# A convolutional LSTM block and a masked bottleneck block on one core: the copy of x1 to the output is issued piece by piece in the last stage

## The reference, cut to what matters

```python
# L0: ConvLSTM over the 96 rows, forward and backward, then a 1x1 projection, batch norm, ReLU
hs_f = _convlstm_scan(xr, w_f[:, :, 1, :], b_f, reverse=False)
hs_b = _convlstm_scan(xr, w_b[:, :, 1, :], b_b, reverse=True)
y = einsum('oc,bchw->bohw', w_proj, concat([hs_f, hs_b]))
x1 = relu(gamma * (y - mu) * rsqrt(var + EPS) + beta) + x       # (8, 48, 96, 96) float32
# L1: masked, channel-pruned inverted bottleneck with a residual
mask = (conv1x1(x1, w_mask) + b_mask >= 0);  mask_dilate = maxpool3x3(mask)
s = sigmoid(mean(x1) @ w_sal.T + b_sal);  vector = (s >= 144th largest of s)   # per image
h = relu(bn1(conv1x1(x1, w_pw1))) * mask_dilate * vector
h = relu(bnd(dwconv3x3(h, w_dw))) * mask * vector
h = bn2(conv1x1(h, w_pw2)) * mask
return x1 + h
```

## Time and profile before

| | |
|---|---|
| median of 3 runs | 1809.51 us (1807.85 to 1809.67) |
| the profiled execution | 1802.15 us, its span 1800.4 us |
| DVE busy over the span | 1397.2 us (78%) |
| PE busy over the span | 1627.0 us (90%) |
| last matmul of `gather` ends | 1229.2 us |
| first matmul of `bottleneck` starts | 1239.2 us |
| first depthwise tap on DVE | 1248.1 us |
| last masked result on DVE | 1789.3 us |
| four copies of x1, issue to landing | 15.7 to 55.1 us |

### The profile page before, as it was taken

The page is one execution under the profiler, slowest core; times in us unless marked ns, Lnnn a source line. Parts: engine busy times, 40 slices in busy tenths (PEclk is TensorE's granted clock), DMA queues, the critical chain, the costliest instruction groups (busy, mean ns, idle before and its releaser), DMA issues. The chain is left out here.

```text
span 1800.4 us, 43798 instructions
## 1 busy us (share of the span) xinstructions
PE 1627.0 (90%) x16562; PEld 1218.2 (68%) x16562; DVE 1397.2 (78%) x2211; ACT 1275.1 (71%) x2343; POOL 54.4 (3%) x88
## 2 busy tenths in 40 slices
PE   5999999999999999999997663457999999999996
PEld 5999999999999999999997221124333333333332
DVE  4777777777777777777776445764999999999996
ACT  4888888888888888888887343703666666666663
POOL 2000000000000000000000000000000000000000
PEclk9999999999999999999999998657999999999997
DMA  4454545455555555555553998929222222222222
GB/s 119 135 143 135 144 134 144 135 143 135 143 136 142 136 141 137 141 138 140 138 139 88 257 256 186 227 67 335 52 45 45 45 45 45 46 46 46 46 46 46
DMA packets 82904, 219.03 MB, mean 122 GB/s; under 512 B 20792, under 2 KB 26828, under 8 KB 82380
## 3 DMA queue, kind: packets, MB, share of 16 engines
q1 hardware_dynamic: 74504, 193.89, 39.7%
q0 software_dynamic: 6144, 16.52, 6.4%
q10 hardware_dynamic: 2180, 7.57, 1.9%
HBM read 98.71 MB, written 61.49 MB: 89 GB/s over the span
## 5 line engine op out<-in xcount | busy, mean ns | idle before, releaser
L1384 DVE SCALAR_TENSOR_TENSOR acc<-h1d,wt,acc 128x768 f32<-128x768 f32 x480 | 483.4, 1017 | 30.5 <-ACT acc L1295 17.3
L264 PE MATMUL gates<-state,w_high 64*128 64x384 f32 x4608 | 504.6, 337 | 0.0
L264 PEld LDWEIGHTS gates<-state,w_high 64*128 64x128 f32 x4608 | 416.8, 185 | 0.0
L1162 PE MATMUL psd<-h1p,wt 64*64 64x384 f32 x3456 | 301.2, 488 | 11.3 <-ACT h2p L1327 11.3
L264 PE MATMUL gates<-state,w_low 64*128 64x384 f32 x2304 | 267.7, 337 | 0.0
L264 PE MATMUL gates<-x_both,w_high 64*128 64x384 f32 x2304 | 237.4, 338 | 18.8 <-DVE w_low L380 18.8
L1162 PEld LDWEIGHTS psd<-h1p,wt 64*64 64x64 f32 x3456 | 126.2, 132 | 187.4 <-issue 173.3
L264 PEld LDWEIGHTS gates<-x_both,w_high 64*128 64x128 f32 x2304 | 207.6, 186 | 18.8 <-issue 18.8
L317 ACT ACTIVATE sig_f<-gates 48x384 f32<-48x384 f32 x384 | 187.0, 487 | 37.9 <-PE gates L264 33.1
L264 PEld LDWEIGHTS gates<-state,w_low 64*128 64x128 f32 x2304 | 208.8, 185 | 0.0
L411 DVE TENSOR_TENSOR h_new<-sig_o,tanh_c 128x384 f32<-128x384 f32 x192 | 107.2, 558 | 122.3 <-ACT tanh_c L335 122.3
(11 more groups left out here) (139 smaller groups left out, 1551.4 us busy)
## 6 DMA issues: line engine op xcount, KB each, us to landing
x_taps<-x_both SPq DMA_DIRECT2D x192, 195.5 KB, 3.1
x_raw<-x_steps SPq DMA_DIRECT2D x192, 192.0 KB, 3.1
h_rows<-h_new SPq DMA_DIRECT2D x192, 144.0 KB, 2.3
h_in<-h_rows SPq DMA_DIRECT2D x48, 576.0 KB, 7.4
x_last<-x_both SPq DMA_DIRECT2D x192, 98.0 KB, 2.9
out<-y SPq DMA_DIRECT2D x4, 4032.0 KB, 36.6
out<-z POOLq DMA_DIRECT2D x48, 336.0 KB, 4.9
sig_o<-x_steps SPq DMA_DIRECT2D x190, 48.0 KB, 2.0
```

The costliest lines, as they stand in the source:

```text
L264: return nc.tensor.matmul(gates[p][d][:, m, 0:NH], w[own, n, m, :], moving[own], start=start, stop=stop)
L1162: mm = nc.tensor.matmul(psd[64 * m:64 * m + 64, i, 0:NH], wt[own, to:to + 64], h1[own, dy + 4 * m:dy + 4 * m + 4, dx:dx + W], start=(tap = ...
L1384: nc.vector.scalar_tensor_tensor(a, window(h1d[d % 2], tap), par(D_UNITS[s], TAP + tap), a, ALU.mult, ALU.add).then_inc(acc_done if tap == ...
```

## The change

The four copies leave `gather`. In `bottleneck` SP issues, behind the two mask transfers of each group, the copy of x1 of this same group and chunk: 8 rows of two images, 112 partitions by 768 values, 336 KB. There are 48 of them. Each pair of images has one semaphore; from the second chunk on SP waits for the pair's copy before, and POOL waits for the copy of its own group in every chunk instead of only in the first. Only pass 0 does so.

```diff
@@ gather, sync
             n = sp.value_load(passes[0:1, 0:1], min_val=1, max_val=2)
-            for g, pair in enumerate(GROUPS):
-                sp.dma_start(out_lanes[:, pair * PX:(pair + 1) * PX],
-                             y[0:HI + C, pair].rearrange("p r w -> p (r w)")).then_inc(copied[g], 16)
             with sp.If(n > 1):
@@ bottleneck, sync, masks(o)
                         sp.dma_start(mask[n % 2][64 * half:64 * half + C], every).then_inc(mask_in[n % 2], 16)
+                    if o == 0:
+
+                        if c:
+                            sp.wait_ge(x1_copied[g], 16 * c)
+                        at = c * CPX
+                        sp.dma_start(out_lanes[:, GROUPS[g] * PX + at:GROUPS[g] * PX + at + CPX],
+                                     y[0:HI + C, GROUPS[g]].rearrange("p r w -> p (r w)")[:, at:at + CPX]
+                                     ).then_inc(x1_copied[g], 16)
@@ bottleneck, gpsimd
                     pool.wait_ge(zm_done, Z + n + 2)
-                    if o == 0 and c == 0:
-                        pool.wait_ge(copied[g], 16)
+                    if o == 0:
+                        pool.wait_ge(x1_copied[g], 16 * c + 16)
```

More of the change, by code:

```diff
@@ L817, in marks_pe, with gather @@
         return 2 + B
-def gather(nc, cst, par, w1, place, folded, wt, packs, packs_stored, passes, y, out_lanes, copied):
+def gather(nc, cst, par, w1, place, folded, wt, packs, packs_stored, passes):
     ORDER = [pair + HB * half for pair in range(HB) for half in range(2)]
@@ L1008, in _, with bottleneck @@
                 program(1)
-def bottleneck(nc, y, out_lanes, wt, packs, passes, copied, mask_rows, masks_stored):
+def bottleneck(nc, y, out_lanes, wt, packs, passes, mask_rows, masks_stored):
     NP, ND, NZ = len(P_IMAGES), len(D_UNITS), len(GROUPS)
@@ L1041, in bottleneck @@
         out_added = [sem(f"out_added{n}") for n in range(2)]
+        x1_copied = [sem(f"x1_copied{g}") for g in range(NZ)]
         pw1_done, relu1_done, prod_done, chain, acc_done, relu2_done = (
@@ L1457, in build @@
         packs_stored = ctx.enter_context(nc.semaphore("packs_stored"))
-        copied = [ctx.enter_context(nc.semaphore(f"x1_copied{g}")) for g in range(HB)]
         masks_stored = ctx.enter_context(nc.semaphore("masks_stored"))
@@ L1479, in build @@
             selection(nc, sums, folded, cst, ws, bs, par, loaded, place, passes)
-            gather(nc, cst, par, w1, place, folded, wt, packs, packs_stored, passes, y, out, copied)
-        bottleneck(nc, y, out, wt, packs, passes, copied, mask_rows, masks_stored)
+            gather(nc, cst, par, w1, place, folded, wt, packs, packs_stored, passes)
+        bottleneck(nc, y, out, wt, packs, passes, mask_rows, masks_stored)
 def kernel(x, L0_conv_w_f, L0_conv_b_f, L0_conv_w_b, L0_conv_b_b, L0_conv_w_proj, L0_conv_gamma, L0_conv_beta,
```

## The result

| | before | changed |
|---|---|---|
| median, 20 runs each | 1809.71 us (1805.71 to 1816.45) | 1805.37 us (1794.43 to 1813.42) |
| ratio | | 0.9968, 95% interval 0.9953 to 0.9983 |
| profiled execution, its span | 1802.15, 1800.4 | 1806.29, 1804.5 |

The account below looks back on a forecast made before the run. VectorE bounds the last stage, and TensorE's jump, its code fetch behind the copies, delays its start. Terms -5.6 + 0 + 0 + 0 + 0 took 1809.5 to 1803.9 us; 8-in-10 range 1799.5 to 1809.0.

Parts of the forecast that it names:

- the hole behind the gather: Between gather and first tap: TensorE idles 10.07 us, seven microseconds its own, its jump's code fetch queued behind the copies' packets.
- Step 1: TensorE's jump at the gather's end: 4.0 us instead of 9.56 once the copies leave, gain 5.6 us (4.7 to 6.6).
- Step 2: Barrier to first tap: TensorE still starts at half clock, taken as 0; catching full clock worth up to 3.1 us.
- rival A: Start of the last stage: TensorE keeps its clock, in all -8.4 us, 1801.1 us; chance 0.18.
- Steps 3 to 5: Last stage: 48 added copies, POOL's wait for its group's copy, and z's later release each cost 0.
- The sum: Whole kernel: -5.6 us with all other terms 0, bounds -9.7 to -4.0, giving 1803.9 us.
- Rival B: TensorE's jump: code fetch waits one packet's turn, or two, so gain only 1.6 to 3.2 us, 1807.1 us; chance 0.13.
- Rival C: TensorE's jump: long because of where it goes, not the copies; change worth 0, 1809.5 us; chance 0.11.
- Rival D: Last stage: copy and accumulating transfer delay each other, z late past 16.9 us landing; slower, 1827 us; chance 0.08.

## Why the prediction was right, point by point

- **What bounds the kernel, and the hole behind the gather.** Right. The jump took 9.6, 10.6, 9.5 and 9.4 us in the four profiles with large copies in flight as it began, and 5.1, 4.7, 4.7, 5.0, 4.8 and once 3.5 in the six without.
- **Step 1, the jump without the copies.** Right in kind, too optimistic in size: I took 4.0 us, the middle of 3.0 and 4.9; the changed kernel measured 5.07 and its repetition 4.99. The gain of the jump was 4.5 us instead of 5.6, the gather's 4.8. The term was mis-sized where I pieced the jump together from a packet of 0.94 us: in the changed kernel two code packets come close behind each other and are served in 1.7 and 2.5 us. With one packet it would have been near the mark: 3.5 us, once. The nearest row was TensorE's own jump at the end, 4.9 us; it should have been the value and not the bound.
- **Step 2, the clock.** The 0 was right, the reasoning was not, so this is partly luck. I had set the pause against the time to the fall as if the length of the pause decided. The clock fell 1.4 to 4.9 us after the last matmul, differently in profiles of like kernels: in the changed kernel after 1.4, sooner than in either case that I had read, without the copies after 4.7. With the shortest pause (2.5 us, second pass left out) the stage began at half clock; in the run with a jump of 3.5 us and a pause of 4.0 the clock held 0.9 us into the stage, and the first tap came 8.1 us behind the barrier instead of 9.5: rival A in small. In the five profiles with a jump of 4.7 to 5.1 us it began at half clock.
- **Steps 3 to 5, the copies in the last stage.** Right: taps 1,019 ns, 540.7 us from the first tap to the last masked result (541 forecast), no new wait, 561.5 us with and 562.1 without copies. Landing grew by 0.8 us where I had allowed 5.
- **The sum.** 1803.9 us forecast, 1805.4 measured; step 1's 1.1 us too much is about that difference, which is itself within the noise. The forecast of -5.6 us lies in the interval, -3.1 to -8.5.
- **Rival B, one packet's turn.** Denied. The code waited 6.4 to 7.2 us in the four profiles with packets of 36 KB, for the rest of one and three more, and 5.3 with 3 KB pieces, of 0.12 us each, where four would be half a microsecond. So the count holds for the large packets only, and what stands in front of the code among small ones stays open. The page "DMA: Bandwidth & Descriptors" of the Trainium skill (section "Queues, rings and completion order") says that a DMA engine changes between queues at packet boundaries and that a packet there is typically 9 to 17 descriptors. I had taken a packet of the profile for such a packet; it may be only a descriptor of one, which no run here shows. What the runs deny is a wait for one of the profile's packets, not that rule.
- **Rival C.** Denied by the repetition and by the copies' move alone (4.7 us).
- **Rival D.** Did not come: 5.7 us of landing where 16.9 would have been needed. A relative of it is real: masks behind large copies in one queue cost 3.4 us in one experiment and 19.8 in another. I had read the 29.3 us of the mask's landing and used it only as an argument for D; it also says why the copies had to be cut when they were moved.

## What to carry to other kernels

Read the drains of a barrier: they name the engine that is late, and an engine that computes nothing can be it. A jump over unused code costs a fetch through the DMA engines, so keep bulk transfers out of its microseconds, and keep them out of the queue in which small urgent ones wait: cut them and issue each behind the urgent one. When stages that did not change vary by more than the change is worth, compare stage by stage and take the total only from many runs.

## What the runs showed of the hardware that I had not expected

- A far jump of TensorE takes 4.7 to 5.1 us (once 3.5) with no copy in flight, and 9.4 to 10.6 us beside large copies, with one of these in flight as with three, and from SP's queue as from ScalarE's. The code stood behind the rest of one packet of 36 KB and three more.
- Issuing can block: eight transfers of 2 MB in 3 KB pieces held SP for up to 9.6 us each, where four of 4 MB in 36 KB pieces took at most 2.2 in the kernel before.
- The end of the kernel has two lengths. In three profiles the last stage took 559.5 to 559.8 us instead of 560.9 to 562.6. VectorE waits less before the last masked result when TensorE has its full clock there, as in the repetition of the kernel before (2.57 us; the earlier trace rows had 4.66, with the clock at 0.50 from 1786 to 1790):

```profile
1798.00:1800.00 2.00, 2.00 (x12) 0.65 (x8) 0.00 (x0) 0.00 (x0) 0.72 (x1) 1.00 0.55 47
```

```profile
1800.17 1.02 DVE L1393 SCALAR_TENSOR_TENSOR z<-ps,wt,mask 128x768 f32<-128x768 f32 x1 [2.57 <-PE ps L1195]
```
